# Softmax sums moved from TensorE to GpSimd adds, value matmuls by query halves, later zero rows, a router on raw tokens, and a norm applied by ScalarE

## The chip, the cores and the metric

One core of a Trainium2 chip runs the program. The metric is the device time of one execution in microseconds (us). Five engines work side by side and wait for one another through semaphores: TensorE (PE: matmuls, PEld: its weight loads), VectorE (DVE), ScalarE (ACT), GpSimd (POOL) and SyncE (SP, which here only issues DMAs).

## What is computed

The input x is 2 x 128 x 32 x 32 (batch, channels, pixels), everything in float32. With L = 1024 pixels per batch item:

```python
x = group_norm(x)                                  # 16 groups, then 1x1 conv to q, k, v
attn = softmax(q @ k / sqrt(128))                  # 4 heads of 32, 1024 x 1024 scores each
x = out_conv(attn @ v) + bias + x
t = tokens(x)                                      # 1024 tokens of 128 channels per batch item
n1 = layer_norm(t)
t = t + linear_attention(n1)                       # 8 heads, keys softmax over tokens, queries over 16 channels
n2 = layer_norm(t)
probs = softmax(n2 @ Wr + br); top 2 of 8 experts
n3 = layer_norm(n2)                                # second norm of each token
y_e = gelu((n3 * g_e + b_e) @ W1_e + b1_e) @ W2_e + b2_e
t = t + weighted sum of the two chosen y_e
```

## The kernel before, in words

**Head (0 to 57 us).** Group norm, q, k, v. Scores need more than one pass of the fast float32r format, so q and k are split into a high and a low part and stacked by DMA into `Qs` and `Ks` (96 rows; two more rows of `Qs` hold minus the row maximum, in two parts, so that the score matmul subtracts it). The maxima come first: a "slot" is one pair (128 queries, one head). `max_first` and `max_second` (L708 to L759) compute its two halves of 512 keys, ScalarE relus one of them (`above`, L529), DVE folds the two into a maximum (`max_slot`, L1066; the fused instruction is L1081). After 8 slots (one unit half k) DVE splits the maxima into `mhl` (L1090, L1091), PE transposes them (L752), DVE copies them (L1073), and SP writes them into `Qs` (L339, `mrow_in[k]`). There are 72 slots with the transposes counted; 13 are done ahead, the other 59 are spread over the first 32 steps, two in 27 steps and one in 5 (`slots_by`, L249). All slots after the first 13 share one pair of PSUM banks, so slot g+1 can only be written when DVE has read slot g.

**Attention steps (64 of them).** Step s handles 128 keys against 512 queries of two heads. The order on PE in step s is: first half of a slot, scores of step s+1 (L775, two matmuls of 512 columns), slots, a part of layer 1 if one is due, then the values of step s (L794). `values` issues four matmuls with 32 output columns each: two heads times {v, ones}. The `ones` matmuls give the softmax sums, in PSUM partitions 64 to 127 of bank 6 or 7. ScalarE makes `probs` (L536, 128 x 1024) into a ring of three. After 8 steps DVE transposes the sums, takes reciprocals and multiplies (`norm_sums`, `norm_reciprocal`, `norm_product`, L1094 to L1110).

**Layer 1 of batch item 0** is cut into named parts, and the table `LAYER1_AT` (L263) says in which step each part is issued, on every engine: residual 33, project 34, statistics and tokens 35, keys 39, and so on to attend 50, norm 52, tokenT 54, logits 56, route 58, counts and norm2 60. `LAYER1_AT_TILE` (L268) does it for batch item 1 between the expert tiles. `norm_stats` (L1113) takes mean and variance, POOL's `rsqrt` (L412, L416) makes the reciprocal root with a power, `norm_apply` (L1122, L1125) applies it with eight DVE instructions of 128 x 128. `v_norm2` (L1195) applies the second norm so, from `F` into `X2`.

**Zero rows.** POOL fills a tile with zeros (L454) and writes it twice over the DRAM buffer of the experts' input (L460, 1.5 MB each) once `mhl_ready` is 1, so that unused rows are harmless. The tile of zeros overlays `t2` and `X2`.

**Experts.** POOL scatters the tokens of a batch item (L473, 16 indirect DMAs) into 23 tiles of 128 rows, SP loads them (L365), and each tile passes PE (transpose L952, two layers L977 and L989), DVE and ScalarE. The results go back by indirect DMAs (L478) and PE combines them (L1010 to L1012). The first nine results are sent before the second scatter.

## Time and profile before

| | |
|---|---|
| median of 3 runs | 394.5 us (392.34 to 397.24) |
| the profiled execution's own time | 393.55 us |
| its span, first to last instruction | 391.8 us |
| mean granted TensorE clock | 0.916 |
| busy: PE, DVE, ACT, POOL | 326.7, 222.2, 187.9, 112.0 us |

The span is what the rows divide; the 1.75 us around it belong to the execution's own time. PE's busy time is of matmuls in flight, which overlap, so a share of 90% does not mean that nothing could be added. POOL's spans are rough. An idle time is put down to what ended it last. Times in the rows are from the start of the span.

### The profile page before, as it was taken

To read this page: it belongs to the slowest core of one execution; us is meant where nothing else is said; L and a number is where in the kernel's file an instruction comes from. 1 tells how busy PE (TensorE), PEld (TensorE's weight loads), DVE (VectorE), ACT (ScalarE), POOL (GpSimd) and SP (SyncE) were. 2 spreads that over 40 slices of the span, in tenths; PEclk is the share of its full clock that TensorE was granted. 3 is DMA by queue.
4 is the path that set the end of the run, shared out by engine and by line. 5 is a ranking of instruction groups with operands and counts; after the bars stand their busy time and mean duration, and the time that the engine had idled before them with its cause. 6 is when DMAs were issued, how large, how long until landed. Compare 5 with 4: busy or idle time off the path is not lost.

```text
span 391.8 us, 6547 instructions
## 1 busy us (share of the span) xinstructions
PE 326.7 (83%) x1970; PEld 208.4 (53%) x1970; DVE 222.2 (57%) x693; ACT 187.9 (48%) x272; POOL 112.0 (29%) x142
## 2 busy tenths in 40 slices
PE   1766739998989989999999878198865998999985
PEld 1433323333433433544524254197865998999985
DVE  2446823456464556264655865376978566888610
ACT  1247115675656665465555511423370465777621
POOL 1086800000000000100011057500371777775420
PEclk9968556999999999999999999869697799999999
DMA  6069495535000000600000001120020214335124
GB/s 183 1 141 228 113 359 119 121 99 212 1 3 1 2 3 27 189 0 2 1 2 0 0 30 47 48 62 22 16 81 8 76 49 125 90 90 160 36 69 173
DMA packets 21773, 29.29 MB, mean 75 GB/s; under 512 B 4055, under 2 KB 15628, under 8 KB 21484
## 3 DMA queue, kind: packets, MB, share of 16 engines
q1 hardware_dynamic: 16828, 18.05, 17.0%
q0 software_dynamic: 3744, 10.31, 8.2%
q10 hardware_dynamic: 1168, 0.52, 0.5%
q8 instruction: 17, 0.28, 0.3%
q14 instruction: 16, 0.13, 0.1%
HBM read 11.62 MB, written 9.25 MB: 53 GB/s over the span
## 4 chain that ended last, share of the span: by engine, by line
PE 57%; DVE 18%; DMA 7%; POOL 7%; issue 6%; SPq 2%; ACT 1%; ACTq 0%; DVEq 0%; POOLq 0%
PE ps L794 13%; PE ps L989 8%; PE ps L977 8%; PE ps L757 6%; POOL expert_in L473 6%; PE ps L775 5%; DVE above L1081 4%; PE ps L737 3%; DMA Qs<-mrow 2%; SPq L331 2%; DMA Qs<-q_hi 2%; DVE pm L1084 2%; DMA attn<-in_L_conv_qkv_weight 1%; PE ps L859 1%; PE ps L693 1%
## 5 line engine op out<-in xcount | busy, mean ns | idle before, releaser
L536 ACT ACTIVATE probs<-ps 128x1024 f32<-128x1024 f32 x64 | 65.3, 1022 | 43.4 <-PE ps L775 43.4
L794 PE MATMUL ps<-probs,vT 128*32 128x512 f32 x256 | 69.2, 617 | 0.1
L794 PE MATMUL ps<-probs,ones 128*32 128x512 f32 x256 | 69.2, 617 | 0.0
L1081 DVE CUSTOM_DVE_ANT_0 above<-ps,above 128x512 f32<-128x512 f32 x56 | 38.7, 691 | 50.3 <-PE ps L757 49.0
L416 POOL TENSOR_TENSOR rstd<-ve,minus_half 128x8 f32<-128x8 f32 (+1 forms) x8 | 11.1, 1385 | 191.5 <-DVE ve L1120 175.2
L989 PE MATMUL ps<-w,GT 128*128 x368 | 52.8, 289 | 7.9 <-ACT GT L637 7.3
L637 ACT ACTIVATE GT<-H 128x512 f32<-128x512 f32 x46 | 29.0, 631 | 57.4 <-DVE H L1342 57.2
L989 PEld LDWEIGHTS ps<-w,GT 128*128 128x128 f32 x368 | 48.0, 204 | 9.6 <-issue 9.5
L977 PE MATMUL ps<-XTT,w1s 128*128 128x128 f32 x368 | 52.4, 289 | 0.0
L529 ACT ACTIVATE above<-ps 128x512 f32<-128x512 f32 x56 | 33.5, 599 | 38.5 <-PE ps L737 38.5
L478 POOL DMA_INDIRECT token_out<-Y,yidx x46 | 44.1, 959 | 22.1 <-DVE Y L1353 14.3
L775 PE MATMUL ps<-Qs,Ks 98*128 98x512 f32 x128 | 44.8, 432 | 6.3 <-DMA Qs<-mrow 6.3
L977 PEld LDWEIGHTS ps<-XTT,w1s 128*128 128x128 f32 x368 | 48.3, 204 | 0.7 <-issue 0.5
L1342 DVE TENSOR_TENSOR H<-ps,b1T 128x512 f32<-128x512 f32 x46 | 31.8, 691 | 23.0 <-PE ps L977 21.9
L473 POOL DMA_INDIRECT expert_in<-X,slots x32 | 31.8, 995 | 35.1 <-DVE X L1125 26.1
L775 PEld LDWEIGHTS ps<-Qs,Ks 98*128 98x128 f32 x128 | 22.4, 195 | 35.3 <-issue 23.5
L757 PE MATMUL ps<-Ks,Qs 96*128 96x512 f32 x64 | 33.2, 519 | 4.7 <-DVE pm L1081 3.0
L757 PEld LDWEIGHTS ps<-Ks,Qs 96*128 96x128 f32 x64 | 13.7, 213 | 37.0 <-DVE pm L1081 30.7
L618 ACT ACTIVATE w1s<-w 128x512 f32 x46 | 28.6, 622 | 0.4
L737 PE MATMUL ps<-Kd,Qs 96*128 96x512 f32 x56 | 25.8, 461 | 0.2 <-DVE pm L1084 0.2
L794 PEld LDWEIGHTS ps<-probs,vT 128*32 128x32 f32 x256 | 9.8, 109 | 20.8 <-issue 17.1
L952 PE MATMUL ps<-ident,XR 128*128 128x128 f32 x46 | 13.6, 295 | 7.7 <-issue 6.5
(185 smaller groups left out, 426.1 us busy)
## 6 DMA issues: line engine op xcount, KB each, us to landing
expert_in<-zeros POOLq DMA_DIRECT2D x2, 1495.0 KB, 8.1
XR<-expert_in SPq DMA_DIRECT2D x46, 65.0 KB, 1.9
Qs<-q_hi SPq DMA_DIRECT2D x16, 128.0 KB, 3.4
w<-in_L_ffn_W SPq DMA_DIRECT2D x1, 2048.0 KB, 8.2
w<-in_L_ffn_W SPq DMA_DIRECT2D x8, 256.0 KB, 4.5
YG<-token_out SPq DMA_DIRECT2D x8, 256.0 KB, 4.2
Ks<-k_hi SPq DMA_DIRECT2D x14, 128.0 KB, 3.1
X<-in_x SPq DMA_DIRECT2D x2, 512.0 KB, 5.0
```

The costliest lines, as they stand in the source:

```text
L473: pool.indirect_dma_start(xs[:, :], bass.IndirectOffsetOnAxis(ap=slots[:, b, w, j:j + 1], axis=0), X2[:, b, j, :], None).then_inc(scattere ...
L478: pool.indirect_dma_start(yt[:, :], bass.IndirectOffsetOnAxis(ap=yidx[:, t:t + 1], axis=0), Y[:, t % NBY, :], None).then_inc(y_sent[t % NB ...
L529: nc.scalar.activation(above[:, n % 2, :], bank(slot_banks(g)[1]), ACT.Relu).then_inc(above_ready, 1)
L536: nc.scalar.activation(probs[:, s % 3, :], bank(2 + 2 * (s % 2), 2), ACT.Exp).then_inc(exp_done, 1)
L737: nc.tensor.matmul(bank(slot_banks(g)[1]), q, Kd[0:SPLIT, b, n, :], start=True, stop=True).then_inc(diff_ready, 1)
L757: last = nc.tensor.matmul(o, Qs[0:SPLIT, b, n, t * P:(t + 1) * P], Ks[0:SPLIT, b, n, HALF:L], start=True, stop=True)
L775: last = nc.tensor.matmul(bank(2 + 2 * (s % 2) + hd), Ks[0:STACK, b, n, kt * P:(kt + 1) * P], Qs[0:STACK, b, n, qh * HALF:(qh + 1) * HALF] ...
L794: last = nc.tensor.matmul(bank(6 + o % 2)[i * HD:(i + 1) * HD, :], w, probs[:, s % 3, hd * HALF:(hd + 1) * HALF], start=kt == 0, stop=kt = ...
L977: last = nc.tensor.matmul(bank(2 + s % 2)[:, c * P:(c + 1) * P], w1s[:, s % 2, c, :], XTT[:, s % NB, :], start=True, stop=True)
L989: last = nc.tensor.matmul(bank(4 + p)[:, 0:D], GT[:, p, c, :], w2[:, e, c, :], start=c == 0, stop=c == HC - 1)
L1081: nc.vector.tensor_tensor_reduce(above[:, n % 2, :], bank(base), above[:, n % 2, :], scale=1.0, scalar=-3.0e38, op0=ALU.add, op1=ALU.max, ...
L1342: nc.vector.tensor_tensor(H1[:, s % NB, :].rearrange("p (c t) -> p c t", c=HC), bank(2 + s % 2).rearrange("p (c t) -> p c t", c=HC), b1T[: ...
```

## The change

- **Sums.** The `ones` matmuls leave `values`. POOL adds the `probs` of four steps (a quad) with three TENSOR_TENSOR adds of 128 x 1024 (`add_probs`; the last quad has one), 46 adds in all. PE multiplies each quad sum by `ones` (`sums_of`), 8 matmuls of 256 columns after every 8 steps, 16 at the end. The ring of `probs` goes from 3 to 5 buffers, and an exponential also waits for the add that reads its buffer's old content.
- **Values** are four matmuls of 256 columns: two query halves times two heads, each on its own 32 output partitions. Their results fill all 128 partitions of 256 columns, and the sums the other 256 columns of the bank; the DVE work after 8 steps is on [128, 256] and comes one step later.
- **Zero rows** are written when the first maxima have landed in `Qs` (`mrow_in[0]`), and no longer when `mhl` is ready.
- **Router** from raw tokens: tokenT transposes `t2` and no longer the normed `F`; the router's weights are centred once (`t_centre`, `v_centre`: one matmul, one DVE instruction), and the logits are multiplied by the token's reciprocal root (one more DVE instruction in `v_gates`).
- **Second norm**: DVE makes only minus mean times root (`v_shift`), ScalarE applies it with 8 activations (`a_norm2`).
- **Order**: POOL's three `rsqrt` of batch item 0 stand between adds (`NORMS_AT`), the first scatter stands behind the last add, and the tables move layer 1's last parts earlier.

```diff
+    NPR = 5
+    QUADS = UNITS * 2 * L // P // 4
+    QSPAN = 256
...
+            r = s % NPR
+            if r < 3:
+                return probs[:, r, :]
+            return (probs_a if s < UNITS * STEPS // B else probs_b)[:, r - 3, :]
+        def quad_sum(q):
+            return (X[:, 1, :], t2[:, 1, :, :].rearrange("p j c -> p (j c)"),
+                    X2[:, 1, :, :].rearrange("p j c -> p (j c)")[:, 0:L])[q % 3]
...
-        LAYER1_AT = {BEGIN_LAYER1: "residual", 34: "project", 35: "tokens_stats tokens", 39: "keys",
+        LAYER1_AT = {BEGIN_LAYER1: "centre residual", 35: "project", 36: "tokens_stats tokens", 39: "keys",
...
-                     50: "attend stats", 52: "norm stats2", 54: "tokenT", 55: "tokenT_sb", 56: "logits",
-                     57: "gates_exp", 58: "route choose", 60: "counts norm2"}
+                     50: "attend stats", 51: "tokenT", 52: "tokenT_sb norm", 53: "logits stats2",
+                     54: "gates_exp", 55: "shift route choose", 56: "norm2", 57: "counts"}
...
-                          4: "norm", 5: "stats2 tokenT", 6: "tokenT_sb", 7: "logits", 8: "gates_exp",
-                          9: "route choose counts norm2"}
+                          4: "tokenT tokenT_sb norm", 5: "logits stats2", 6: "gates_exp", 7: "shift route choose norm2",
+                          8: "counts"}
+        NORMS_AT = {(8, 3): 0, (12, 2): 1, (13, 1): 2}
+        LAST_QUAD = UNITS * STEPS - 4
+        def added_by(s):
+            return 3 * (s // 4) + max(1, s % 4) if s < LAST_QUAD + 2 else 3 * (QUADS - 1) + 1
...
-            pool.wait_ge(mhl_ready, 1)
+            pool.wait_ge(mrow_in[0], 16 * 2)
...
+            def add_probs(q, i):
+                s = 4 * q + i
+                pool.wait_ge(exp_done, s + 1)
+                if i == 1 and q >= 3:
+                    pool.wait_ge(sum_done, (q - 3) // 2 + 1)
+                if i > 1:
+                    pool.wait_ge(probs_added, added_by(s - 1))
+                nc.gpsimd.tensor_tensor(quad_sum(q), probs_of(s - 1) if i == 1 else quad_sum(q), probs_of(s),
+                                        ALU.add).then_inc(probs_added, 1)
+            pool.wait_ge(resid_ready, B)
+            for q in range(QUADS):
+                for i in range(1, 4 if q < QUADS - 1 else 2):
+                    add_probs(q, i)
+                    if (q, i) in NORMS_AT:
+                        rsqrt(B + NORMS_AT[q, i])
...
-                if s >= 3:
-                    act.wait_ge(pv_done, s - 2)
+                if s >= NPR:
+                    act.wait_ge(pv_done, s - NPR + 1)
+                    act.wait_ge(probs_added, added_by(s - NPR))
...
+            def a_norm2(b):
+                act.wait_ge(nm2_ready, b + 1)
+                for j in range(J):
+                    last = nc.scalar.activation(X2[:, b, j, 0:D], F[:, j, :], ACT.Identity, bias=nm2[:, b, j:j + 1],
+                                                scale=rstd[:, B + 3 * b + 2, j:j + 1])
+                last.then_inc(x2_ready, 1)
...
+                for i in range(2):
+                    for hd in range(2):
+                        n = head(u, hd)
+                        last = nc.tensor.matmul(query_span(o, i)[hd * HD:(hd + 1) * HD, :],
+                                                vT[:, b, kt, n * HD:(n + 1) * HD],
+                                                probs_of(s)[:, hd * HALF + i * QSPAN:hd * HALF + (i + 1) * QSPAN],
+                                                start=kt == 0, stop=kt == KT - 1)
...
+            def sums_of(o):
+                parts = [quad_sum(2 * o), quad_sum(2 * o + 1)]
+                if o < 2 * UNITS - 1:
+                    pe.wait_ge(probs_added, added_by(KT * o + KT - 1))
+                else:
+                    pe.wait_ge(probs_added, added_by(LAST_QUAD))
+                    parts += [probs_of(LAST_QUAD + 2), probs_of(LAST_QUAD + 3)]
...
+            def t_centre(b):
+                if b == 0:
+                    pe.wait_ge(slot_used, SLOTS)
+                    nc.tensor.matmul(ps[:, 0:E], ones[:, :], rw[:, :], start=True, stop=True).then_inc(means_ready, 1)
...
-                pe.wait_ge(n2_ready, b + 1)
+                pe.wait_ge(t2_ready, b + 1)
...
+                values(s)
+                if s % KT == 1 and s > KT:
+                    sums_of(s // KT - 1)
...
-            def v_norm2(b):
-                norm_apply(F, X2[:, b, :, 0:D], B + 3 * b + 2, x2_ready)
+            def v_shift(b):
+                i = B + 3 * b + 2
+                dve.wait_ge(rstd_ready, i + 1)
+                nc.vector.scalar_tensor_tensor(nm2[:, b, :], lmv[:, :, 0], -1.0, rstd[:, i, :], ALU.mult,
+                                               ALU.mult).then_inc(nm2_ready, 1)
```

## Rows read from the trace of the kernel before

The groups stand in the order in which the prediction comes to them.

**Rows 1.** Stretches: span, busy us (count) of PE, PEld, DVE, ACT, POOL; PEclk, DMA
```profile
57.00:66.00 9.00, 9.00 (x25) 4.23 (x29) 2.10 (x6) 5.10 (x7) 0.29 (x2) 0.50 0.77 182
66.00:152.80 86.80, 80.03 (x404) 31.11 (x396) 46.19 (x130) 54.09 (x78) 0.00 (x0) 1.00 0.17 50
152.80:226.50 73.70, 71.30 (x446) 30.46 (x445) 43.62 (x159) 37.79 (x40) 4.96 (x3) 1.00 0.10 29
```

**Rows 2.** The chain of waits, head of the attention: start us, us, what
```profile
49.01 7.90 DMA Qs<-mrow
```

**Rows 3.** Timeline of POOL and SP there, and two rows of the DMA issues
```profile
48.01 1.15 POOL L460 DMA_DIRECT2D expert_in<-zeros  x2 [0.54 <-POOL zeros L455]
...
48.31 1.57 SPq L339 DMA_DIRECT2D Qs<-mrow  x2
...
expert_in<-zeros POOLq DMA_DIRECT2D x2, 1495.0 KB, 8.1
XR<-expert_in SPq DMA_DIRECT2D x46, 65.0 KB, 1.9
```

**Rows 4.** Timeline of a step with two slots: start us, us, engine, line, what
```profile
143.95 0.62 PE L794 MATMUL ps<-probs,vT 128*32 128x512 f32 x1
...
144.95 0.50 PE L757 MATMUL ps<-Ks,Qs 96*128 96x512 f32 x1
...
145.48 0.69 DVE L1081 CUSTOM_DVE_ANT_0 above<-ps,above 128x512 f32<-128x512 f32 x1 [0.96 <-PE ps L757]
...
146.24 0.50 PE L757 MATMUL ps<-Ks,Qs 96*128 96x512 f32 x1
...
147.90 0.50 PE L757 MATMUL ps<-Ks,Qs 96*128 96x512 f32 x1
```

**Rows 5.** Groups by line: the one two-input elementwise instruction on POOL
```profile
L428 POOL TENSOR_TENSOR kd_lo<-kd,kd_hi 128x512 fp32r<-128x512 f32 x2 | 2.6, 1278 | 3.2 <-ACT kd_hi L520 3.2
```

**Rows 6.** Timeline, and the instructions of L1090 (ns min/median/max)
```profile
44.61 2.59 POOL L454 MEMSET zeros<- 128x2990 f32 x1
...
45.03 2.20 DVE L1090 TENSOR_SCALAR mhl<-pm 128x8 fp32r<-128x8 f32 x1
...
L1090 DVE TENSOR_SCALAR mhl<-pm x8: 170/172/2196, 45.0 to 152.1; 128x8 fp32r<-128x8 f32 x8
```

**Rows 7.** Timeline: a POOL instruction beside a DVE one with two SBUF inputs
```profile
248.04 1.23 DVE L1158 TENSOR_TENSOR QV<-QV,qst 128x1024 f32<-128x1024 f32 x1
248.26 1.84 POOL L473 DMA_INDIRECT expert_in<-X,slots  x1 [0.30 <-issue]
```

**Rows 8.** The chain of waits, layer 1 of batch item 0
```profile
161.46 0.99 PE ps L794 x8
162.45 0.67 PE ps L775 x2
...
169.75 1.72 PE ps L833 x4
...
196.93 1.73 PE ps L877 x4
...
202.61 1.66 POOL rstd L416
204.30 2.15 DVE F L1125 x8
```

**Rows 9.** Timeline, expert tiles: PE behind the second norm; DVE at the scatter's end
```profile
303.44 1.22 PE L989 MATMUL ps<-w,GT 128*128 x4 [3.49 <-ACT GT L637]
...
321.50 0.69 DVE L1342 TENSOR_TENSOR H<-ps,b1T 128x512 f32<-128x512 f32 x1 [0.62 <-PE ps L977]
...
323.34 0.69 DVE L1342 TENSOR_TENSOR H<-ps,b1T 128x512 f32<-128x512 f32 x1 [0.50 <-PE ps L977]
...
325.63 0.69 DVE L1342 TENSOR_TENSOR H<-ps,b1T 128x512 f32<-128x512 f32 x1 [0.95 <-PE ps L977]
...
329.05 0.69 DVE L1342 TENSOR_TENSOR H<-ps,b1T 128x512 f32<-128x512 f32 x1 [0.65 <-PE ps L977]
```

More of the change, by code:

```diff
@@ L148, in build_program @@
         lmv = sb("lmv", [P, J, 2])
+        nm2 = sb("nm2", [P, B, J])
         pm = sb("pm", [P, 2, 2, QH])
@@ L778, in scores, with values @@
                     last.then_inc(st_ready, 1)
-            def values(u, step, hd):
-                s = u * STEPS + step
-                b, qh, kt = u // PAIRS, step // KT, step % KT
-                o = 2 * u + qh
-                if hd == 0:
-                    pe.wait_ge(exp_done, s + 1)
-                    if kt == 0:
-                        if o >= 2:
-                            pe.wait_ge(o_used, o - 1)
-                        else:
-                            pe.wait_ge(slot_used, AHEAD)
-                n = head(u, hd)
-                for i, w in ((hd, vT[:, b, kt, n * HD:(n + 1) * HD]), (2 + hd, ones[:, 0:HD])):
-                    last = nc.tensor.matmul(bank(6 + o % 2)[i * HD:(i + 1) * HD, :], w,
-                                            probs[:, s % 3, hd * HALF:(hd + 1) * HALF],
-                                            start=kt == 0, stop=kt == KT - 1)
-                if hd:
-                    last.then_inc(pv_done, 1)
+            def values(s):
+                u, step = s // STEPS, s % STEPS
+                b, kt = u // PAIRS, step % KT
+                o = s // KT
+                pe.wait_ge(exp_done, s + 1)
+                if kt == 0:
+                    if o >= 2:
+                        pe.wait_ge(o_used, o - 1)
+                    else:
+                        pe.wait_ge(slot_used, AHEAD)
+                for i in range(2):
[5 more added lines that the diff above has]
+                                                start=kt == 0, stop=kt == KT - 1)
+                last.then_inc(pv_done, 1)
@@ new lines, in sums_of @@
+            def sums_of(o):
+                parts = [quad_sum(2 * o), quad_sum(2 * o + 1)]
+                if o < 2 * UNITS - 1:
+                    pe.wait_ge(probs_added, added_by(KT * o + KT - 1))
+                else:
+                    pe.wait_ge(probs_added, added_by(LAST_QUAD))
+                    parts += [probs_of(LAST_QUAD + 2), probs_of(LAST_QUAD + 3)]
+                if o >= 2:
+                    pe.wait_ge(o_used, o - 1)
+                for n, part in enumerate(parts):
+                    for i in range(2):
+                        for hd in range(2):
+                            r = (2 * i + hd) * HD
+                            last = nc.tensor.matmul(bank(6 + o % 2)[r:r + HD, QSPAN:2 * QSPAN], ones[:, 0:HD],
+                                                    part[:, hd * HALF + i * QSPAN:hd * HALF + (i + 1) * QSPAN],
+                                                    start=n == 0, stop=n == len(parts) - 1)
+                last.then_inc(sum_done, 1)
@@ L934, in _ @@
                 run_parts(layer1, LAYER1_AT, s, 0)
-                for hd in range(2):
-                    values(s // STEPS, s % STEPS, hd)
+                values(s)
+                if s % KT == 1 and s > KT:
+                    sums_of(s // KT - 1)
                 for g in new[1:2]:
@@ L1107, in norm_product @@
                 b, pair = u // PAIRS, u % PAIRS
-                place = attn[64 * pair:64 * pair + 64, b, :].rearrange("c (j p) -> c p j", j=J)[:, qh * 64:(qh + 1) * 64, :]
-                nc.vector.tensor_tensor(place, bank(6 + o % 2)[0:64, :].rearrange("c (p j) -> c p j", j=J),
-                                        rec[:, :].rearrange("c (p j) -> c p j", j=J), ALU.mult).then_inc(o_used, 1)
+                place = attn[64 * pair:64 * pair + 64, b, :].rearrange("c (j p) -> c p j", j=J)
+                for i in range(2):
+                    at_ = qh * 64 + i * 32
+                    last = nc.vector.tensor_tensor(place[:, at_:at_ + 32, :],
+                                                   query_span(o, i).rearrange("c (p j) -> c p j", j=J),
+                                                   rec[64 * i:64 * i + 64, :].rearrange("c (p j) -> c p j", j=J), ALU.mult)
+                last.then_inc(o_used, 1)
             def norm_stats(src, i):
@@ L1286, in _ @@
                 o = s // KT - 1
-                closing = s % KT == 1 and s > KT
+                closing = s % KT == 2 and s > KT
                 for g in new[0:1]:
```

63 lines of the change are left out of this document (44 added, 19 removed).

## The prediction, written before the changed kernel was seen

> **What bounds the kernel now.** I read three views in this order. The stretches of the span [rows 1] show where PE is the bound. From 66.0 to 152.8 us, where two slots of maxima ride on almost every attention step, PE is busy 80.0 of 86.8 us at a granted clock of 1.00. From 152.8 to 226.5 us, where layer 1 of batch item 0 rides on the steps, it is busy 71.3 of 73.7 us. POOL is busy 0.0 and 5.0 us in these two stretches, so there is an idle engine beside a full one. Then the chain of waits shows what starts the attention: a DMA of 16 KB in all that takes 7.90 us [rows 2]. Then the timelines give the inside of a step. Where two slots are due, the step is 147.90 - 144.95 = 2.95 us long [rows 4]: one slot goes from L757 over DVE to the next L757 in 146.24 - 144.95 = 1.29 us, and the second takes 1.66 us because the values stand between. In the second stretch a plain step is 0.99 us of values and 0.67 of scores, 1.66 us, back to back on PE [rows 8].
>
> **The change, part by part.** All terms are against the profiled execution, 393.55 us (span 391.8 and 1.75 around it). It stands 0.95 us under the median of 394.5, well inside their spread, so I carry its sum over unchanged.
>
> *Zero rows.* POOL issues them from 48.01 us, just ahead of the maxima's DMAs of SP (48.31, issued by 49.88), and they land 8.1 us after their issue; the maxima's DMA, released at 49.01, ends with them at 56.91 [rows 2, 3]. Written later, they can't be ahead of it. A small SP load lands 1.9 us after its issue [rows 3], so 49.88 + 1.9 = 51.8 instead of 56.9: **-5.1**. Bounds: -6 (nothing at all in the way) and -2 (the stack loads issued from 50 us on are what held it). Moved, the 3 MB run from 52 to about 61 us. What they now delay is POOL's first add and the loads of units 2 and 3, first needed some ten steps later. An exponential first needs an add in step 5, at about 67 us, and that add is done by about 65.
>
> *Values, steps with slots.* The two passes of values start 0.45 us apart (143.95 and the end of the group at 144.95, which is two passes and 0.1 of drain) [rows 4]. Half the columns are then half of it: 0.45 us less per step. In a step with two slots the saving is cut short, because the slot path of 2 x 1.29 = 2.58 us becomes the bound: 2.95 - 2.58 = 0.37. With 27 such steps and 5 with one slot: 27 x 0.37 + 5 x 0.45 = **-12.2**. Bounds: -14.4 (32 x 0.45) and -6, if matmuls of 256 columns keep a larger fixed part.
>
> *Sums on PE.* Eight matmuls of 256 columns per 8 steps are 0.9 us by the same rate. Three times in the first stretch, where PE (2.5 us of each step) has no room: **+2.7**.
>
> *What POOL's adds cost.* The one add-like instruction of POOL takes 1278 ns for 512 columns [rows 5]; for 1024 I take 2.45 us with its start, between 2.2 (part of it fixed) and 2.8. With 46 adds that is 113 us on an engine that idles there. Three adds per four steps are 1.84 us per step, under the 2.58 of the first stretch, but over the 1.21 us (0.67 + 0.54) that PE would need for a plain step in the second. GPSIMD Engine Reference, Performance versus the Vector engine, of the Trainium skill measures 4497 ns for a float32 add of 2048 columns; by half of that the 46 adds would be 103 us, an estimate that changes no term here.
>
> *POOL against DVE, first stretch.* `mhl` (L1090) normally takes 0.17 us. In one of its eight places it took 2.20, and it ended at 47.23, when POOL's memset of 2.59 us from 44.61 ended at 47.20 [rows 6]. So such a DVE instruction waits for a POOL one to finish. From now on an add is running for 7.35 of every 10.3 us. Seven later `mhl` stand on the slot path, and each waits half an add in 71% of cases: 7 x 0.87 = **+6.1**. Bounds: 0, and 7 x 2 x 2.45 = 34 if L1090 and L1091 each wait for a whole one.
>
> *Second stretch without such waits.* From the end of the project matmuls (161.46) to the keys (169.75) there were 8.3 us [rows 8]. Now it is the chain copy, statistics, root, norm, about 7.7 us, since four steps of 1.21 are shorter; centring before it (a matmul and a DVE instruction, both ways waited for, 0.9 us) and one sum (0.9) come on top: +1.1. From the keys to the end of attend (198.66), 11 steps give 11 x 0.45 = 5.0, and two sums (1.8) and a wait for the key exponentials (0.9) take 2.7 back: -2.2. From there to the end of the steps 27.8 us passed. POOL now has nine adds there (22.1), two roots of 1.66 [rows 8] and a wait for statistics of about 2.5, together 27.9, and the first scatter stands behind them in POOL's order: 0. The transposes from raw tokens remove a PE wait of 1.2 us that this bound hides anyway. Sum **-1.1**, bounds -12 (PE alone the bound) and +6. ScalarE's norm, 8 activations, delays one exponential by about 3 us in step 56, inside these bounds.
>
> *POOL against DVE, second stretch.* Some twelve DVE groups read two SBUF tensors or are of L1090's kind: the two norms, the query subtraction and scaling, and the router's small ones. That two SBUF inputs matter too is seen at 248.26 us, where a POOL instruction of 0.96 us took 1.84 while DVE's L1158 (two SBUF inputs) ran until 249.27 [rows 7]. Half an add in 70% of cases is 10 us, of which I put half on the path: **+5**, bounds 0 and +22 (nine whole adds).
>
> *Expert stage.* The second norm of item 1 leaves DVE. Its like takes 2.15 us [rows 8], and PE waited 3.49 us behind that block [rows 9]: -2.1. The second scatter can start earlier: tiles that came every 1.84 us (321.50, 323.34) came 2.29 and 3.42 us apart at its end [rows 9], 2.0 us that go. The last sums (1.8 us for 16 matmuls) are paid by DVE being free sooner at the end of the attention and by shorter transposes. Sum **-4.1**, bounds -9 and +2.
>
> **The sum.** -5.1 - 12.2 + 2.7 + 6.1 - 1.1 + 5 - 4.1 = -8.7, so 393.55 - 8.7 = 384.9, say **385 us**.
>
> **A rule that speaks against the change.** Rows 6 show one DVE instruction held to the end of a POOL one, rows 7 the reverse. The Trainium skill, SBUF — State Buffer, Who interferes with whom, says that the shared port pair is an exclusive lock: the later of the two "fully blocks" for the whole instruction, for two-port DVE modes, and for DVE instructions with two SBUF inputs against a POOL instruction that reads SBUF. The trace agrees in both rows. If the pair also changes hands between the eight instructions of a norm, this is the slower rival below.
>
> **The rivals.**
> 1. *The waits between DVE and POOL hardly reach the path* (DVE keeps the pair through a row of instructions, or its instructions fall into POOL's gaps). For it: seven of eight `mhl` ran in 0.17 us, and only a busy POOL makes the eighth; against it: POOL will be busy. Without the 6.1 and the 5: 393.55 - 19.8 = 374 us.
> 2. *Slower: every contending DVE instruction waits for a whole add*, because POOL has a backlog and takes its turn between any two of them. Place: `mhl` and its second instruction, then the eight of each norm (up to three adds each are ready), then the router. Price: 7 x 2.4 = 17 and 9 x 2.45 = 22 us, 393.55 - 19.8 + 39 = 413 us. It decides the sign once more than 19.8 us of such waits, eight whole adds, are on the path. For it: rows 6 show a wait to the very end. Against it: in the first stretch POOL follows the exponentials and has little backlog.
> 3. *The slot instruction itself (L1081) waits for the adds.* It reads PSUM and one SBUF tensor. Then DVE's 1.4 and POOL's 1.84 us per step run one after the other, 3.3 us a step instead of 2.95: +11 instead of -3.4, so 399 to 400 us. No row of before has a reading POOL beside it; rows 7 only show two SBUF inputs.
> 4. *The clock.* After the wait of 6 us for the maxima PE ran at 0.50, the lower level of 1.2 GHz, for the 9 us from 57 to 66 [rows 1]. If PE's new waits at the keys or the counts bring one or two such falls in the second stretch, 4.5 us are lost in each: 392 us. Against it: the waits expected there are 3 to 5 us.
>
> **How the numbers follow.** The forecast has 0.42 (own range 378 to 393), the first rival 0.25, the second 0.15, the third 0.08, the fourth 0.10. The lower end, 370, takes in all but the lower tail of the first rival; the upper, 405, all but most of the second. That leaves out somewhat under 0.2. What a measurement can tell is about 2%, 7.9 us, so faster means under 386.6 and slower over 402.4. Faster: 0.24 of the forecast, nearly all of the first rival and 0.02 of the fourth, 0.50. Slower: the second and a little of the third and the forecast, 0.18. The same: 0.32.
>
> **What would show each step.** The first scores start at 52 us and not at 57. A step with two slots is 2.6 us long, and values take 0.55 us of PE. An add takes 2.4 to 2.5 us. L1090 shows a spread between 0.17 and 2.6 us, and its mean says which rival holds; so do the norms' rows of eight, which stay at 2.15 us each if DVE keeps the pair and grow to 5 to 9 us if not. L1081 stays at 0.69 us, or the third rival is true. In the second stretch ScalarE's exponentials should be released by POOL as often as by PE. The second scatter starts some 6 us sooner against the first tile. The forecast is wrong if the first stretch is not about 3 us shorter, if the second differs from 74 us by more than 7, or if PE's clock falls in it.

## The result, and the profile after

The changed kernel takes 429.1 us (median of 4 runs, 424.23 to 431.25) against 395.9 us for the kernel before (4 runs), a ratio of 1.081 with an interval of 1.068 to 1.095: **slower by 8%**, 33 us. The forecast was 385 us, its range ended at 405, and its slowest rival stood at 413. Ratios, here and below, leave out disturbed executions, which are some per cent longer at a lower granted clock, so they can differ a little from the quotient of the medians; of the profiles below only that of `pow` is of such an execution.

The exponentials of steps 0, 32 and 63 cut the span into comparable parts. The first exponential starts at 58.2 us before and at 51.8 after. Columns of the rows: stretch, its length, busy us (count) of PE, PEld, DVE, ACT and POOL, then PEclk, DMA share and GB/s. The kernel before, exp 0 to 32, exp 32 to 63, and the rest:

```profile
58.20:151.90 93.70, 87.67 (x422) 34.24 (x421) 47.75 (x133) 58.30 (x85) 0.29 (x2) 0.96 0.22 60
151.90:224.30 72.40, 69.37 (x433) 30.21 (x437) 42.06 (x153) 37.67 (x39) 4.96 (x3) 1.00 0.10 30
224.30:391.80 167.50, 137.59 (x1026) 125.87 (x1026) 104.81 (x363) 74.69 (x128) 80.93 (x81) 0.92 0.23 69
```

The same stretches of the changed kernel:

```profile
51.80:161.80 110.00, 97.62 (x470) 46.13 (x469) 54.73 (x138) 60.20 (x85) 57.48 (x26) 0.72 0.26 79
161.80:260.80 99.00, 72.23 (x499) 37.00 (x503) 60.67 (x163) 40.37 (x48) 57.11 (x25) 0.76 0.08 22
260.80:428.00 167.20, 140.50 (x1058) 128.48 (x1050) 99.36 (x344) 77.72 (x136) 81.12 (x83) 0.91 0.23 69
```

So the span grows by -6.4 (head: the 6.4 us by which the attention starts sooner) + 16.3 + 26.6 - 0.3 = 36.2 us, all of it in the attention steps. Three columns carry the story. PE's idle time (length less busy) goes from 6.0 to 12.4 and from 3.0 to 26.8 us. DVE's busy time grows by 7.0 and 18.6 us though it has only 5 and 10 instructions more. And PEclk falls from 0.96 and 1.00 to 0.72 and 0.76.

**The head** did what was forecast. The maxima's DMA (two of 4 KB, so 8 KB and not the prediction's 16), 7.90 us long in [rows 2], is short, and the first scores start at 50.5 us (the chain of waits; below it, from the waits and the timelines, what the zero rows then hold up: start us, us, engine, line):

```profile
48.73 1.75 DMA Qs<-mrow
...
65.85 0.14 POOL L495 IOTA X<- 128x8 f32 x1 [13.67 <-DMA expert_in<-zeros]
...
66.33 2.37 POOL L506 TENSOR_TENSOR X<-probs 128x1024 f32<-128x1024 f32 x1 [0.34 <-POOL X L495]
...
68.81 1.02 ACT L589 ACTIVATE probs<-ps 128x1024 f32<-128x1024 f32 x1 [1.91 <-POOL X L506]
...
70.38 0.50 PE L798 MATMUL ps<-Kd,Qs 96*128 96x512 f32 x1 [1.76 <-ACT above L577]
```

The zero rows were issued by 52.2 and POOL waited for them until 65.8, where the forecast had them done at 61. The first add came late, exp 5 waited for it, ScalarE's slot work stood behind that, and PE waited 1.8 us. It is the only exponential that POOL released: 43 others waited for PE.

**DVE and POOL.** The add takes 2.37 us (forecast 2.45, [rows 5]). `mhl`, 0.17 us in seven of eight places in [rows 6], is now held for nearly a whole add in four of them (L1176 at 76.3, 107.9 and 123.3 us, L1177 at 142.8). It looks like this (timelines of POOL, DVE and PE around 108 us, then the two instructions' own rows, ns min/median/max):

```profile
107.72 2.36 POOL L506 TENSOR_TENSOR t<-probs 128x1024 f32<-128x1024 f32 x1 [3.21 <-ACT probs L589]
...
107.91 2.20 DVE L1176 TENSOR_SCALAR mhl<-pm 128x8 fp32r<-128x8 f32 x1
...
111.02 0.28 PE L813 MATMUL ps<-ident,mhl 128*16 128x128 f32 x1 [2.12 <-DVE pm L1167]
...
L1176 DVE TENSOR_SCALAR mhl<-pm x8: 171/460/2305, 46.2 to 161.7; 128x8 fp32r<-128x8 f32 x8
L1177 DVE SCALAR_TENSOR_TENSOR mhl<-pm,mhl x8: 166/168/2292, 47.0 to 161.9; 128x8 fp32r<-128x8 f32 x8
```

The add ends at 110.08 and `mhl` at 110.11: the small instruction waits for the end of the add that was running. The norm's eight instructions, 2.15 us together in [rows 8], fare worse, and the router's chain waits one instruction at a time (timelines):

```profile
182.65 2.33 POOL L506 TENSOR_TENSOR X<-probs 128x1024 f32<-128x1024 f32 x1
182.70 8.20 DVE L1216 TENSOR_SCALAR F<-t,lmv,rstd 128x128 f32<-128x128 f32 x8 [1.78 <-POOL rstd L447]
185.12 4.93 POOL L506 TENSOR_TENSOR X<-X,probs_b 128x1024 f32<-128x1024 f32 x2
...
190.96 2.07 PE L917 MATMUL ps<-F,wT 128*128 128x512 f32 x2 [8.73 <-DVE F L1216]
...
238.33 2.30 DVE L1298 SCALAR_TENSOR_TENSOR nm<-lmv,rstd 128x8 f32<-128x8 f32 x1 [1.76 <-POOL rstd L447]
...
241.04 2.14 DVE L1318 TENSOR_TENSOR lg<-lg,lst 128x64 f32<-128x64 f32 x1
...
245.12 2.17 DVE L1325 CAST topf<-topi 128x16 f32<-128x16 uint32 x1
...
247.71 2.05 DVE L1329 TENSOR_TENSOR wts<-top,lst 128x16 f32<-128x16 f32 x1
...
250.35 0.69 PE L981 MATMUL ps<-mask,upper 128*128 128x64 f32 x2 [10.56 <-DVE mask L1337]
```

Three adds had gathered behind the root (POOL's order puts it between adds), and they took their turns between the norm's instructions, one at a time: three whole adds in one row of eight. In this stretch the sixteen norm instructions take 14.4 us instead of 4.3, and the four small ones above take 8.7 (2.30 + 2.14 + 2.17 + 2.05), where they take 0.74 in the run `short_adds` of the experiments. PE waited 8.7 us for the keys and 10.6 for the mask; in the kernel before its longest wait in this stretch was 1.2 us. Not all of that is the adds' doing: in `short_adds` PE still waits 2.7 and 4.5 us at these two places.

**The slot step** is the forecast's 2.6 us where the clock is full and 3.87 where it is halved (scores' starts: 116.07 - 113.47, and 157.24 - 153.37 = 153.37 - 149.49):

```profile
113.47 0.63 PE L836 MATMUL ps<-Qs,Ks 98*128 98x512 f32 x2
...
116.07 0.63 PE L836 MATMUL ps<-Qs,Ks 98*128 98x512 f32 x2
...
149.49 1.05 PE L836 MATMUL ps<-Qs,Ks 98*128 98x512 f32 x2
...
153.37 1.05 PE L836 MATMUL ps<-Qs,Ks 98*128 98x512 f32 x2
...
157.24 1.05 PE L836 MATMUL ps<-Qs,Ks 98*128 98x512 f32 x2
```

**The clock** fell to 1.2 GHz after several of these waits and not after all of them. After the wait of 2.12 us that ended at 111.0 it stayed full (first row). The other rows lie behind the wait of 2.10 us for `mhl` that ended at 126.4 (low), behind the one of 2.50 us that ended at 146.3 (low), within the wait for the keys (low), behind that (full again), and within the waits for router and mask (low):

```profile
103.40:127.10 23.70, 18.34 (x119) 8.19 (x121) 16.31 (x37) 14.27 (x20) 14.50 (x7) 0.99 0.01 1
127.30:140.70 13.40, 13.40 (x66) 6.44 (x58) 4.20 (x12) 6.27 (x9) 4.75 (x3) 0.52 0.01 2
148.00:170.00 22.00, 20.64 (x79) 11.33 (x80) 6.00 (x20) 9.40 (x12) 11.10 (x5) 0.50 0.21 59
184.00:195.00 11.00, 4.04 (x12) 1.37 (x12) 7.13 (x9) 0.00 (x0) 5.76 (x3) 0.53 0.01 1
196.00:229.00 33.00, 31.06 (x251) 17.98 (x250) 20.54 (x40) 18.91 (x20) 23.76 (x10) 1.00 0.01 1
230.00:256.00 26.00, 11.44 (x64) 4.54 (x60) 22.07 (x84) 7.71 (x14) 12.66 (x6) 0.50 0.00 0
```

L1167, the slot's fold, stays at 0.691 us, so it waits for no add.

### The profile page after: what moved, and what is told of

Its sections match the earlier page's. It is cut to its first block, busy times and chain, and to the rows that moved or that the text cites. A ratio compares the mean times of both kernels' runs of the same rounds, so it can differ in the third digit from the quotient of the medians.

```text
span 428.0 us, 6952 instructions
## 1 busy us (share of the span) xinstructions
PE 343.7 (80%) x2116; PEld 230.4 (54%) x2116; DVE 241.0 (56%) x690; ACT 195.5 (46%) x288; POOL 221.1 (52%) x188
## 4 chain that ended last, share of the span: by engine, by line
PE 46%; DVE 17%; issue 14%; POOL 13%; DMA 5%; ACT 2%; SPq 2%; ACTq 0%; DVEq 0%; POOLq 0%
PE ps L1075 7%; PE ps L855 6%; PE ps L1063 6%; POOL expert_in L523 5%; PE ps L818 5%; PE ps L836 5%; PE ps L798 3%; POOL X L506 3%; POOL token_out L528 2%; PE ps L874 2%; DVE above L1167 2%; DVE F L1216 2%; POOL rstd L447 2%; SPq L362 2%; PE ps L754 2%
## 5 line engine op out<-in xcount | busy, mean ns | idle before, releaser
L1167 DVE CUSTOM_DVE_ANT_0 above<-ps,above 128x512 f32<-128x512 f32 x56 | 38.7, 691 | 53.9 <-PE ps L818 50.1
L836 PE MATMUL ps<-Qs,Ks 98*128 98x512 f32 x128 | 54.3, 513 | 0.1
L698 ACT ACTIVATE GT<-H 128x512 f32<-128x512 f32 x46 | 29.0, 630 | 53.8 <-DVE H L1447 53.8
L589 ACT ACTIVATE probs<-ps 128x1024 f32<-128x1024 f32 x39 | 39.5, 1022 | 17.3 <-PE ps L836 15.4
L1447 DVE TENSOR_TENSOR H<-ps,b1T 128x512 f32<-128x512 f32 x46 | 31.8, 691 | 23.8 <-PE ps L1063 19.9
L818 PE MATMUL ps<-Ks,Qs 96*128 96x512 f32 x64 | 39.1, 611 | 3.8 <-DVE pm L1167 2.1
L836 PEld LDWEIGHTS ps<-Qs,Ks 98*128 98x128 f32 x128 | 27.9, 240 | 19.8 <-issue 12.7
L855 PE MATMUL ps<-probs,vT 128*32 128x256 f32 x312 | 31.7, 487 | 4.0 <-ACT probs L589 4.0
L506 POOL TENSOR_TENSOR X<-X,probs 128x1024 f32<-128x1024 f32 x12 | 29.3, 2438 | 10.6 <-ACT probs L589 10.0
L798 PE MATMUL ps<-Kd,Qs 96*128 96x512 f32 x56 | 31.2, 558 | 1.9 <-ACT above L577 1.8
L818 PEld LDWEIGHTS ps<-Ks,Qs 96*128 96x128 f32 x64 | 16.6, 259 | 27.7 <-DVE pm L1167 22.9
L589 ACT ACTIVATE probs_b<-ps 128x1024 f32<-128x1024 f32 x13 | 13.3, 1023 | 21.7 <-PE ps L836 21.7
L1216 DVE TENSOR_SCALAR F<-t,lmv,rstd 128x128 f32<-128x128 f32 x32 | 19.0, 664 | 5.4 <-POOL rstd L447 5.4
```

The costliest lines, as they stand in the source:

```text
L506: nc.gpsimd.tensor_tensor(quad_sum(q), probs_of(s - 1) if i == 1 else quad_sum(q), probs_of(s), ALU.add).then_inc(probs_added, 1)
L589: nc.scalar.activation(probs_of(s), bank(2 + 2 * (s % 2), 2), ACT.Exp).then_inc(exp_done, 1)
L798: nc.tensor.matmul(bank(slot_banks(g)[1]), q, Kd[0:SPLIT, b, n, :], start=True, stop=True).then_inc(diff_ready, 1)
L818: last = nc.tensor.matmul(o, Qs[0:SPLIT, b, n, t * P:(t + 1) * P], Ks[0:SPLIT, b, n, HALF:L], start=True, stop=True)
L836: last = nc.tensor.matmul(bank(2 + 2 * (s % 2) + hd), Ks[0:STACK, b, n, kt * P:(kt + 1) * P], Qs[0:STACK, b, n, qh * HALF:(qh + 1) * HALF] ...
L855: last = nc.tensor.matmul(query_span(o, i)[hd * HD:(hd + 1) * HD, :], vT[:, b, kt, n * HD:(n + 1) * HD], probs_of(s)[:, hd * HALF + i * QS ...
```

## The experiments

The theory: adds hold up DVE, DVE holds up PE, and the clock falls after PE's waits. Its parts are how an add holds DVE (by its length, or by being busy at all), and whether the lighter values let the clock fall. Three chips were used, numbered here 1 to 3. On chip 1 the kernel before took 395.3 us, on chips 2 and 3 it took 417.4. The difference lies behind the last exponential: one and the same kernel (`rest` and `rest_b`) needs 165.5 us there on chip 1 and 186.0 on chip 3, while its attention steps take 169.3 and 169.7. So totals are told as ratios to the kernel before on the same chip, and stretches are compared for the attention alone.

| run | what it is | ratio, interval | exp 0 to 32, 32 to 63, us | chip |
|---|---|---|---|---|
| after | the change | 1.081, 1.068 to 1.095 | 110.0, 99.0 | |
| short_adds | adds of 8 columns | 1.001, 0.996 to 1.006 | 97.0, 79.4 | 1 |
| twice | values twice | 1.081, 1.073 to 1.089 | 107.1, 102.7 | 1 |
| zeros_late | before + late zero rows | 0.987, 0.979 to 0.994 | 92.1, 72.5 | 1 |
| rest | + router, second norm | 0.981, 0.975 to 0.988 | 92.8, 76.5 | 1 |
| short_twice | short adds, values twice | 1.022, 1.018 to 1.027 | 99.8, 81.8 | 2 |
| quarters | each add in four | 1.039, 1.034 to 1.043 | 98.2, 90.5 | 2 |
| pow | powers for adds | 1.012, 1.009 to 1.016 | (104.0, 79.1) | 2 |
| early | change, zero rows early | 1.085, 1.078 to 1.092 | 107.1, 99.0 | 3 |
| early_short | same, short adds | 1.013, 1.009 to 1.018 | 93.6, 75.4 | 3 |
| mixed | router, second norm for item 1 only | 0.978, 0.974 to 0.983 | 92.2, 72.6 | 2 |
| mixed_b | `mixed` again | 0.979, 0.976 to 0.983 | 92.8, 72.6 | 3 |
| rest_b | `rest` again | 0.980, 0.976 to 0.984 | 94.2, 75.5 | 3 |

(The profiled execution of `pow` took 430.3 us, its others 422 to 424; its stretches stand in brackets and only its durations on DVE and POOL are used.)

### Are the adds' columns the cause: short_adds, early, early_short

`short_adds` keeps every add, wait and order and cuts the adds to 8 of 1024 columns, so most of the sum is left out and the sums are wrong; the rest of the tiles is filled with ones, three memsets of 0.95 us ahead of the first add.

```diff
-                nc.gpsimd.tensor_tensor(quad_sum(q), probs_of(s - 1) if i == 1 else quad_sum(q), probs_of(s),
-                                        ALU.add).then_inc(probs_added, 1)
+                nc.gpsimd.tensor_tensor(quad_sum(q)[:, 0:8], (probs_of(s - 1) if i == 1 else quad_sum(q))[:, 0:8],
+                                        probs_of(s)[:, 0:8], ALU.add).then_inc(probs_added, 1)
...
+            for q in range(3):
+                link(nc.gpsimd.memset(quad_sum(q), 1.0))
```

> The changed kernel with GpSimd's 46 adds cut from 1024 to 8 columns (the sums are then of three tiles filled with ones beforehand; everything else, PE's light values included, stays). Theory W (waits): TensorE's clock falls because PE is left waiting 2 to 3 us behind DVE instructions that GpSimd's adds hold up. Without long adds L1090's counterpart is back at 0.17 us and the norm's eight at 2.1 us, the clock stays at 1.00 from about 66 us to the first scatter, steps with two slots take 2.6 us, and the whole 370 to 378 us. Theory L (light work): the clock falls because the values matmuls with half the columns leave PE too little to do. Then it still falls in the stretch with slots, which keeps 5 to 8 of its 16 us over the kernel before, and the whole is 385 to 395 us.

Measured: 397.5 us, ratio 1.001. So the adds' length is worth the 8%. The time lies above what either theory had (370 to 378, 385 to 395): with short adds the first stretch still takes 3.3 us more than before and the second 7.0 more. PE still waits 3.6 us at exp 5, 2.7 at the keys and 4.5 at the mask, and the clock falls four times (at about 71, 139, 173 and 217 us).

`early` and `early_short` are the changed kernel and `short_adds` with the zero rows back in their old place, run side by side:

```diff
-            pool.wait_ge(mrow_in[0], 16 * 2)
+            pool.wait_ge(mhl_ready, 1)
```

> The changed kernel with its zero rows put back to where they were (after the first folded maximum, ahead of the first maxima's input). Theory (after's first add stands behind the zero rows, whose landing took 14 us, exp 5 waits for that add, and the wait costs 4 us and a fall of the clock): first exp at 58 instead of 51.8 us, no wait of TensorE at exp 5, exp 0 to exp 32 103 to 107 us instead of 110; time 426 to 431 us where after has 429, so putting the zero rows late is worth little in this kernel. Rival (the late zero rows are worth here what they are worth alone, 5 us): 434 to 436 us.

> The kernel with short adds (8 of 1024 columns, wrong sums, ones elsewhere), its zero rows put back to where they were. No long adds and no wait at exp 5. Theory (what short adds left is the clock falling after a wait, the first of them exp 5's): exp 0 to exp 32 90 to 93 us (97.0 with the zero rows late), time 396 to 400 us, ratio near 1.00. Rival (the falls come without that wait, or at other waits of the closing steps just as often): exp 0 to exp 32 96 to 98 us, time 401 to 404 us, ratio 1.012 to 1.02.

Measured on one chip: 456.0 and 423.5 us. The same two stretches of `early`,

```profile
57.30:164.40 107.10, 94.27 (x470) 44.12 (x469) 55.06 (x138) 59.72 (x85) 57.11 (x25) 0.75 0.20 53
164.40:263.40 99.00, 72.21 (x499) 36.98 (x503) 60.65 (x163) 40.31 (x48) 57.03 (x26) 0.76 0.08 22
```

and of `early_short`:

```profile
57.20:150.80 93.60, 87.76 (x470) 40.99 (x469) 46.32 (x136) 59.25 (x85) 7.80 (x28) 0.82 0.22 60
150.80:226.20 75.40, 64.76 (x499) 33.73 (x503) 41.54 (x165) 40.28 (x47) 11.12 (x26) 0.93 0.10 29
```

With almost the same instruction counts DVE is busy 8.7 and 19.1 us less, PE idles 7.0 and 16.2 us less (12.8 to 5.8, 26.8 to 10.6), and the stretches are 13.5 and 23.6 us shorter. The totals differ by 32.5 us, about the whole loss of the change, on one chip and with the order of the instructions kept.

The side question was exp 5's wait. In `early` the first exponential comes at 57.3 and the first stretch is 2.9 us shorter than after's: the ratio of 1.085 (430 us in terms of a before of 395.9) is not to be told from after's 1.081. So with long adds the late zero rows bring little; the theory for `early` held, though its interval reaches 432 us in the same terms, close to the rival's 434. In `early_short` the wait at exp 5 is gone, and yet the clock fell at about 92 us: the row of 92.00:108.00 has PEclk 0.50 with PE busy 15.9 of 16 us. A wait of 1.3 us ended at 90.8; behind the same wait at 94.9 us `short_adds` kept the full clock. The stretch, 93.6, lies between the two expectations, and the ratio is the rival's (1.012 to 1.02). The wait at exp 5 was gone and a fall came all the same, at a later one.

### Length or columns: quarters, pow

`quarters` makes each add in four adds of 256 columns. `pow` has, for each short add, a power over 12 columns, which keeps POOL busy and moves little (the sums are left out as in `short_adds`):

```diff
-                nc.gpsimd.tensor_tensor(quad_sum(q), probs_of(s - 1) if i == 1 else quad_sum(q), probs_of(s),
-                                        ALU.add).then_inc(probs_added, 1)
+                nc.gpsimd.tensor_tensor(quad_sum(q)[:, 0:12], quad_sum(q)[:, 0:12], quad_sum(q)[:, 0:12],
+                                        ALU.pow).then_inc(probs_added, 1)
```

> The changed kernel with each GpSimd add made as four adds of 256 columns. Theory 1 (a VectorE instruction of the kind that waits, waits for the end of the one GpSimd instruction in progress): the folded maximum (2.3 us at most in the changed kernel) takes 0.8 us at most, the norm's eight (8.2 us) take 5 to 7, exp 0 to exp 32 falls from 110 to 103-106 us, exp 32 to exp 63 from 99 to 85-93, time 408 to 420 us. Rival 1 (what counts is how long GpSimd is busy, its pace or a share of the port): four pieces take longer than one (2.6 to 3 us against 2.37), the sum of the waits stays, time 427 to 440 us. Rival 2 (the first add's wait for the zero rows and the clock after it carry the loss): 426 to 431.

> As with short adds (wrong sums: ones stay in the tiles), but in place of each short add a power over 12 columns, which keeps GpSimd busy for about as long as the full add (a power over 8 columns took 1.66 us) while it reads and writes hardly anything. Theory 1 (VectorE waits for the whole GpSimd instruction, whatever it moves): folded maxima of 0.5 to 2.3 us again, stretches near 110 and 99 us, time 425 to 432. Rival (only the traffic of a 1024-column add stands in the way): folded maxima 0.17 to 0.3, stretches near 97 and 79, time 396 to 402.

`quarters`: ratio 1.039, so half of the loss is gone; in terms of a before of 395.9 that is 411 us, in the first theory's range. Its adds take more POOL time than the whole ones (4 x 0.73 to 0.75, some 2.95 us against 2.37), so POOL's pace is not what costs. The folded `mhl` takes 0.77 us at most and the norm 5.08 instead of 8.20 (its timeline and the instruction's own row):

```profile
172.50 5.08 DVE L1220 TENSOR_SCALAR F<-t,lmv,rstd 128x128 f32<-128x128 f32 x8 [1.79 <-POOL rstd L447]
...
L1220 DVE TENSOR_SCALAR F<-t,lmv,rstd x32: 333/470/771, 172.5 to 295.3; 128x128 f32<-128x128 f32 x32
```

The longest norm instruction was 2402 ns after and is 771 here: the wait is as long as one POOL instruction, and there are more of them. The first stretch came out better than forecast (98.2 for 103 to 106).

`pow`: ratio 1.012 (401 us in the same terms), which is the rival's value. One of the groups of POOL by line, the timelines where powers and norm meet, and the row of `mhl` (its 2253 ns are the place beside the memset of zeros at 44.9 us, as in [rows 6]):

```profile
L506 POOL TENSOR_TENSOR X<-X 128x12 f32<-128x12 f32 x31 | 70.4, 2271 | 31.4 <-ACT probs L591 16.7 <-ACT probs_a L591 7.6 <-ACT probs_b L591 5.7
...
176.92 7.08 POOL L506 TENSOR_TENSOR X<-X 128x12 f32<-128x12 f32 x3
...
176.99 2.14 DVE L1218 TENSOR_SCALAR F<-t,lmv,rstd 128x128 f32<-128x128 f32 x8 [1.75 <-POOL rstd L447]
...
L1178 DVE TENSOR_SCALAR mhl<-pm x8: 171/172/2253, 44.9 to 155.9; 128x8 fp32r<-128x8 f32 x8
```

Three powers run for 7.08 us, the same place and nearly the same length as after's three adds, and the norm's eight take 2.14 us beside them, as before. Over the two stretches DVE is busy 46.6 and 41.3 us, the same as in `short_adds`, beside a POOL that is busy 57.7 and 53.8 us. Here a POOL busy with powers holds up nothing on DVE; one that adds 1024 columns does. **The theory that DVE waits for the whole POOL instruction, whatever it moves, is refuted.** The Trainium skill, SBUF — State Buffer, section SBUF: two separate sides, says that VectorE and GpSimd share a pair of ports, and that whichever of two contending instructions starts first has the pair for its whole length. The adds agree (110.08 and 110.11 above); the powers don't, and for them the measurement decides. Whether it is the columns or the kind of instruction that frees DVE is not separated: no run has a power over 1024 columns.

`pow` stands 1.1% above `short_adds` (1.012 and 1.001, on two chips), so at most some 4 us can be due to POOL's pace.

### Does the lighter TensorE work matter: twice, short_twice

Both issue every values matmul twice into the same accumulation, so that the values come out doubled; `short_twice` leaves out most of the sums as well.

```diff
+                for again in range(2):
                     ...
-                       start=kt == 0, stop=kt == KT - 1)
+                       start=kt == 0 and again == 0, stop=kt == KT - 1 and again == 1)
```

> The changed kernel with each values matmul issued twice (the result is doubled), so that PE has the columns of the kernel before again; GpSimd's adds stay whole. Theory L: the clock is back at 1.00 in the stretch with slots and the kernel gets faster in spite of more matmuls, 405 to 415 us. Theory W: the waits are still there, so the clock still falls after them, and with the added columns the whole is 430 to 445 us.

> Sums on GpSimd cut to 8 of 1024 columns (wrong sums, the tiles hold ones elsewhere) and every values matmul issued twice, so TensorE has about the columns per slot that it had before, and no long add beside it. Theory 1 (TensorE's lighter work is what lets the clock fall at each wait): the stretches from exp 0 to exp 32 and from exp 32 to exp 63 come back to about 94 and 74 us (before 93.7 and 72.4; 97.0 and 79.4 with short adds and values once), and the time is 387 to 391 us. Rival (the clock falls after any wait, and the falls left with short adds come from waits of the closing steps and the router alone): 97 and 79 us again or more, 397 us or above.

`twice`: 428.0 us, the same as the change (ratio 1.081 for both), between the two expectations, with 718 matmul records in the first stretch for 470. PEclk rises to 0.90 and 0.87:

```profile
51.90:159.00 107.10, 95.33 (x718) 46.05 (x717) 53.21 (x136) 58.90 (x84) 56.82 (x26) 0.90 0.27 82
159.00:261.70 102.70, 81.48 (x747) 42.92 (x751) 61.43 (x165) 40.58 (x48) 58.52 (x26) 0.87 0.07 22
```

The waits stay, a little shorter: 1.73, 1.74 and 2.08 us at `mhl` for 2.12, 2.10 and 2.50. The clock fell behind two of these three, as in the changed kernel, but it was full again after about 4 and 7 us, and there only after some 14 and 23. What the clock gives back the columns take. The granted clock over the span shows it in every execution: 0.81 to 0.82 with the change, 0.89 to 0.90 with the values twice.

`short_twice`: after the fall that follows exp 5's wait (3.5 us, in `short_adds` 3.6) the clock stays full for 140 us, while `short_adds` has its falls at 139 and 173 us and later. `short_twice`:

```profile
80.00:220.00 140.00, 131.26 (x1199) 68.51 (x1197) 71.12 (x239) 77.87 (x104) 12.64 (x39) 1.00 0.11 35
```

`short_adds`:

```profile
85.00:139.00 54.00, 48.69 (x311) 22.53 (x311) 31.55 (x92) 36.27 (x53) 2.82 (x15) 1.00 0.14 50
140.00:160.00 20.00, 19.11 (x94) 11.05 (x94) 4.28 (x14) 7.29 (x9) 0.80 (x4) 0.52 0.35 103
```

With the columns put back the clock is higher; that much is shown. But the waits are shorter too where `short_adds` has its falls: 0.7 us for 1.1 before the first, and 0.95 at the keys for 2.7 before the second. How much is the columns' own doing and how much the shorter waits' is not separated. The time forecast (387 to 391, ratio near 0.985) is a miss: the ratio of 1.022 and the stretches of 99.8 and 81.8 us are the rival's, though the clock is not. Steps at full clock are 2.97 us again (exp 13 to 32: 95.8 to 152.3), and the waits at exp 5 (3.5 us), at the mask (2.9) and in the closing steps remain. Halving the columns is still worth something without long adds, 1.0% between `short_twice` (1.022) and `pow` (1.012) on one chip, but not the 3% forecast (12.2 us), and with long adds nothing: lighter steps run slow in parts, heavier ones run full.

### What the other parts are worth: zeros_late, rest, mixed

`zeros_late` is the kernel before with the one line of `early` the other way round. `rest` adds the router from raw tokens, the shifted tables and the second norm by ScalarE; sums and values stay on PE. `mixed` has late zero rows too, and the router from raw tokens and the second norm by ScalarE for batch item 1 alone.

```diff
-            pool.wait_ge(mhl_ready, 1)
+            pool.wait_ge(mrow_in[0], 16 * 2)
```

> The kernel before with nothing changed but the zero rows written when the first maxima have landed. In the changed kernel the first exponential came 6.4 us sooner. If that is this part's doing and nothing takes it back, 387 to 390 us (6 us less than before). Rival: the loads that the zero rows now delay are waited for later, or the 0.50 clock at the start lasts longer, and it is within 2 us of before.

> The kernel before with all of the change but the sums and the values: late zero rows, router from raw tokens, second norm by ScalarE, and the shifted parts of layer 1 (project and statistics stay at steps 34 and 35). Without adds GpSimd holds nothing up. My theory: the 6 us of the zero rows and 3 to 5 us of the second norm and the earlier second scatter, 382 to 387 us; so the whole loss of the change comes from the sums and values. Rival: ScalarE's eight activations and the waits for raw statistics give the second part back, 387 to 391 us.

> The kernel before with the zero rows behind the first maxima's input, and raw tokens for the router and the second norm by ScalarE for item 1 alone (item 0 as before, router weights centred at step 61); sums and values by TensorE as before. Theory (the two parts pay where they stand in the expert stage and cost where they stand in the slot steps): exp 0 to exp 63 takes 164.6 us as with the zero rows alone, the rest after exp 63 165.5 us as with both parts on both items, time 384 to 386 us. Rival (item 1's gain came only from the second scatter being issued earlier after item 0's, so it goes): 388 to 390.

> The same kernel as mixed, beside rest_b on one chip. Theory (the second norm by ScalarE and the raw tokens cost 4 us in the slot steps and give 5 us in the expert stage): exp 0 to exp 63 164.6 us against 169.3 with rest_b, time 3 to 5 us under rest_b's, ratio 0.970 to 0.978. Rival (they are worth the same either way): the two within 1 us of one another.

> The same kernel as rest, beside mixed_b on one chip. Ratio 0.978 to 0.985 by either theory; by the first, 3 to 5 us above mixed_b, by the rival, within 1 us.

`zeros_late`: 390.0 us, 5.3 under the kernel before, as the -5.1 of the prediction. First exponential at 52.1, stretches of 92.1 and 72.5 as before, nothing given back: without adds nobody waits for the zero rows. `rest`: 387.8 us, 2.1 less, intervals that overlap, as its rival had it (387 to 391). In its profile the attention takes 4.7 us more (169.3 against 164.6) and the part behind it 5.4 less (165.5 against 170.9; the kernel before, whose work there is the same as that of `zeros_late`, took 167.5, so 3 us of this can be noise). `mixed` has the short attention forecast for it (164.8 us for 164.6), but came to 0.978, 387 us in terms of a before of 395.9, between its theory (384 to 386) and its rival (388 to 390). `mixed_b` has the short attention, 165.4 against 169.7 of `rest_b`, and the part behind it is 1.1 us longer; yet the medians of six runs are 409.1 and 409.2. The profiled executions say 3 us, the runs say none, as the rival of `mixed_b` had it; the first theory is not confirmed, and taking the parts apart by batch item brought nothing measurable. The best kernels here are `rest` and `mixed`, 2% under the kernel before and, by the ratios, some 9% under the change.

## Why the prediction was wrong, step by step

All three of the prediction's signs that it is wrong came: the first stretch is 16.3 us longer and not 3 shorter, the second takes 99.0 us and not about 74, and the clock falls in it.

- **Zero rows, -5.1:** right alone (5.3); in the head of the changed kernel it was -6.4, just outside its bound of -6. What was wrong was the cover: "that add is done by about 65" rested on the zero rows landing at 61. They landed at 65.8, and the add ended at 68.7. In the whole no run shows anything left of the 5.3 us: `early`, without this part, is at 1.085 for 1.081.
- **Values, -12.2, and sums, +2.7:** the step of 2.6 us at full clock was right, and the add at 2.37 us. What failed is that the clock would be full.
- **`mhl` behind adds, +6.1:** the sum was right, its form was not, so this is partly luck. It was to be half an add in 71% of seven places; four places waited for nearly a whole one and three for none, and three of the four made PE wait, 6.7 us together. In all PE idles 6.4 us more in the first stretch, 1.8 of it behind exp 5.
- **The clock in the first stretch was left out. This is the first step that failed.** The forecast let rival 4 act in the second stretch alone and against two falls of 4.5 us. PEclk 0.72 over 110.0 us means 0.56 of them, 62 us, at the lower level; at 3.87 us a step for 2.6 that costs 62 x 0.33 = 20 us, an estimate, against 2.5 before (0.96 over 93.7). Of the +16.3 us, +6.4 are idle time and +18 the clock, which leaves 8 us of saved work for the 9.5 forecast. `twice` shows that the change itself, by its lighter steps, takes part in it: PEclk 0.90 for 0.72.
- **POOL against DVE in the second stretch, "half an add in 70% of cases is 10 us, of which I put half on the path: +5". This is the second step that failed.** DVE's extra busy time there is 18.6 us, and PE idles 23.8 us more; the adds' share of that is 16.2 (`early` against `early_short`), three times the +5. The wait was not half an add in a fraction of cases: POOL had a backlog of adds where the norm and the router stood, so instruction after instruction waited for a whole one. That is the mechanism of rival 2, priced there at 22 us, which had 0.15 and a total of 413. It was right in the second stretch and too high in the first (17 us for 6.7), and its 413 lacked the clock.
- **Rival 3** is false, L1081's successor stays at 0.691. **Rival 1** is false: the waits reached PE. The sign that exponentials would be released by POOL as often as by PE failed, one against 43: POOL's pace was not the bound that the second stretch was reckoned by.
- **Second stretch without waits, -1.1:** can't be read apart from the waits; with short adds the stretch is 75.4 to 79.4 us for 72.4 before, so it was too good by 4 to 8. The waits for the keys (2.7 us) and the mask (4.5), which stay with short adds, are the part that it had too small; before, the longest wait in this stretch was 1.2 us.
- **Expert stage, -4.1:** -0.3 measured, within the 3 us by which this stage differs between `before` and `zeros_late`. The wait for the first tile's load is 1.2 us shorter (5.3 for 6.5), but that for the first tile behind the second scatter is 3.2 longer (4.1 for 0.9). This scatter starts 1.4 us sooner against the first tile, and not the 6 of the prediction's sign. Why was not tried.

## What to carry to other kernels

Work given to an idle GpSimd can be paid for by VectorE: here each add of 1024 columns could hold one VectorE instruction for its whole 2.4 us. Count which VectorE instructions stand in rows or chains where GpSimd has a backlog, and price each at one whole GpSimd instruction; if it must be there, cut it into pieces and keep the backlog away from the chains. And where TensorE is the bound at full clock, what is gained by taking matmul columns away can be lost to the clock when short waits come in with the same change: price every new wait with the steps that run slow behind it (here 3.87 us for 2.6).

## What the runs showed of the hardware that was not expected

- An add of 1024 columns (2.37 us) keeps DVE's norm waiting, 8.20 us for eight instructions; powers over 12 columns (2.27 us each, three in 7.08 us) don't, 2.14 us. How long GpSimd is busy is not what counts.
- Beside an add of the changed kernel waited DVE's tensor_scalar, scalar_tensor_tensor, tensor_tensor and cast between SBUF tiles (the small ones 0.17 to 0.34 us alone, 2.05 to 2.40 held). Not held were the fused fold and other instructions that read PSUM, transposes, reciprocals and index searches (L1167 0.691 us beside adds and without).
- Between two of eight DVE instructions issued back to back a waiting add gets its turn, and one add's turn is as long as the instruction: at most 2402 ns with whole adds, 771 ns with quarters.
- With the values issued twice the time did not change (428.0 against 429.1 us): PEclk went from 0.72 and 0.76 to 0.90 and 0.87. Behind waits of about 2 us the low level lasted 4 and 7 us, and 14 and 23 with half the columns.
- Chips differ by 22 us in the kernel before (395.3 on one, 417.4 on two others); in `rest`, which was profiled on chips 1 and 3, 20.5 us of the difference lie behind the last exponential. On chip 3 PE has two waits of 8.5 us between expert tiles there; on chip 1 none of its waits in that part is over 5.5 us.
